# Three multiplications of the second attention on VectorE as two-tensor operations

## The reference

```python
def _L1_xattn_ref(latents, context, Wq, Wk, Wv, Wo, q_norm_w, k_norm_w):
    kv = jnp.concatenate([context, latents], axis=1)          # 64 + 256 keys
    q = (latents @ Wq).reshape(bsz, q_len, HEADS, HEAD_DIM).transpose(0, 2, 1, 3)
    k = (kv @ Wk).reshape(bsz, kv_len, KV_HEADS, HEAD_DIM).transpose(0, 2, 1, 3)
    v = (kv @ Wv).reshape(bsz, kv_len, KV_HEADS, HEAD_DIM).transpose(0, 2, 1, 3)
    q = rms_norm(q, q_norm_w)
    k = rms_norm(k, k_norm_w)
    qg = q.reshape(bsz, KV_HEADS, groups, q_len, HEAD_DIM)
    scores = jnp.einsum('bhgqd,bhkd->bhgqk', qg, k) * scale
    probs = jax.nn.softmax(scores.astype(jnp.float32), axis=-1).astype(q.dtype)
    out = jnp.einsum('bhgqk,bhkd->bhgqd', probs, v)
    ...
    return out @ Wo
```

## Time and profile before

| what | value |
|---|---|
| median of three runs | 1533.31 us (1529.5 to 1533.53) |
| profiled execution, first to last instruction | 1532.8 us |
| PE busy | 1433.3 us, 94% |
| DVE busy | 1135.0 us, 74% |
| ACT busy | 756.9 us, 49% |
| POOL busy | 517.1 us, 34% |
| mean granted TensorE clock | 0.990 |

### The profile page before, as it was taken

One profiled execution on the slowest core, in us unless ns is written; L12 is line 12 of the kernel. 1 busy time (PEld: TensorE's weight loads), 2 busy tenths in 40 slices (PEclk: granted clock), 3 DMA queues, 4 the chain that ended last, 5 costly groups with the idle time before them and its releaser, 6 DMA issues. The chain is left out here.

```text
span 1532.8 us, 24378 instructions
## 1 busy us (share of the span) xinstructions
PE 1433.3 (94%) x8064; PEld 1209.6 (79%) x8064; DVE 1135.0 (74%) x2870; ACT 756.9 (49%) x2127; POOL 517.1 (34%) x586
## 2 busy tenths in 40 slices
PE   5999999999999998999999999999999999999889
PEld 4888888887778887787888878878878887877767
DVE  7888888888641426778788788787787787786765
ACT  5666666667220314545545554554555555455521
POOL 4733333443691722232132132132132222322110
PEclk9999999999999999999999999999999999999979
DMA  4111111120230300100101001001001001010001
GB/s 186 70 66 45 68 55 68 68 68 1 83 112 28 131 18 1 69 1 15 56 1 68 0 0 68 0 0 68 0 0 68 0 0 68 19 35 1 1 1 55
DMA packets 14933, 63.75 MB, mean 42 GB/s; under 512 B 1760, under 2 KB 1760, under 8 KB 10656
## 3 DMA queue, kind: packets, MB, share of 16 engines
q1 hardware_dynamic: 14880, 63.07, 11.6%
HBM read 60.97 MB, written 2.10 MB: 41 GB/s over the span
## 5 line engine op out<-in xcount | busy, mean ns | idle before, releaser
L1183 ACT ACTIVATE p<-psum,nb,rq 128x320 f32<-128x320 f32 x256 | 155.5, 614 | 208.1 <-DVE nb L997 208.0
L55 PE MATMUL psum<-w1q_hi,xnT_lo 128*128 128x512 f32 x256 | 108.9, 425 | 7.7 <-DVE v_lo L1017 4.3
L993 DVE TENSOR_REDUCE mx<-psum 128x2 f32<-128x640 f32 x128 | 105.0, 820 | 9.4 <-PE psum L57 3.8
L962 DVE TENSOR_TENSOR pT_lo<-psum,pT_hi 128x512 fp32r<-128x512 f32 x128 | 88.0, 688 | 26.1 <-ACT pT_hi L1126 24.0
L923 POOL TENSOR_TENSOR rk<-ssk,rms_eps 128x3 f32<-128x3 f32 x32 | 6.2, 195 | 296.6 <-DVE ssk L1031 296.6
L243 POOL TENSOR_TENSOR p<-p,rinv 128x256 f32<-128x256 f32 x64 | 39.2, 613 | 193.0 <-DVE rinv L319 193.0
L434 ACT ACTIVATE p<-psum,nb 128x64 f32<-128x64 f32 x256 | 76.8, 313 | 50.7 <-DVE nb L344 50.6
L56 PE MATMUL psum<-w1q_lo,xnT_hi 128*128 128x512 f32 x256 | 101.4, 396 | 0.0
L57 PE MATMUL psum<-w1q_hi,xnT_hi 128*128 128x512 f32 x256 | 101.2, 395 | 0.0
L55 PE MATMUL psum<-w1o_hi,oT_lo 128*128 128x512 f32 x256 | 100.9, 394 | 0.0
L56 PE MATMUL psum<-w1o_lo,oT_hi 128*128 128x512 f32 x256 | 100.6, 393 | 0.0
(11 more groups left out here) (249 smaller groups left out, 4827.5 us busy)
## 6 DMA issues: line engine op xcount, KB each, us to landing
raw_q<-in_w0q SPq DMA_DIRECT2D x8, 1024.0 KB, 4.8
raw_o<-in_w0o SPq DMA_DIRECT2D x8, 1024.0 KB, 4.8
raw_q<-in_w1q SPq DMA_DIRECT2D x8, 1024.0 KB, 7.6
raw_o<-in_w1o SPq DMA_DIRECT2D x8, 1024.0 KB, 4.9
raw_kv<-in_w_gu SPq DMA_DIRECT2D x10, 512.0 KB, 3.6
raw_gu<-in_w_gu SPq DMA_DIRECT2D x10, 512.0 KB, 3.6
raw_kv<-in_w0kv SPq DMA_DIRECT2D x8, 515.0 KB, 3.3
raw_kv<-in_w1kv SPq DMA_DIRECT2D x8, 512.0 KB, 5.6
```

Source lines behind the costliest of these rows:

```text
L55: pe.matmul(out, w[1], m[0], start=start, stop=False)
L962: last = dve.tensor_tensor(k.pT[1][:, kt, 2 * hp:2 * hp + 2, :], bank.rearrange("p (h q) -> p h q", h=2), f(k.pT[0][:, kt, 2 * hp:2 * hp + ...
L993: dve.tensor_reduce(k.mx[:, stat(j)], s_pair(j), AX.X, ALU.max).then_inc(mx_ready, 1)
L1183: last = act.activation(k.p1[:, tile, h, :], s_pair(j)[:, h % 2, :], ACT.Exp, bias=k.nb[:, i:i + 1], scale=k.rq[:, i:i + 1], accum_out=k.r ...
```

## The change

Three things on DVE in attention 1. The maximum is reduced with its sign turned (`negate=True`, tile `neg_mx` in place of `mx`), and its product with `rq` is a tensor_tensor of two elements in place of a scalar_tensor_tensor. The two tensor_scalar operations of 320 elements that scale a pair of heads of p become one tensor_tensor of 640 elements with `rinv` repeated along the keys (`over_keys`). The two or three tensor_scalar operations of 128 elements on `k_raw` become one tensor_tensor of 256 or 384 elements with `rk` repeated. POOL's `p_scale` is written with the same helper and does what it did. Waits, semaphore counts and the order of the work stay.

```diff
--- before.py
+++ after.py
@@ -810,7 +810,7 @@
     k.p1 = sb(scope, "p1", [2, GH, SEQ + CTX])
     k.dump, k.rms_eps = sb(scope, "dump", [2 * GH + 3, HD]), sb(scope, "rms_eps", [2 * GH])
     k.ssk, k.rk = sb(scope, "ssk", [3]), sb(scope, "rk", [3])
-    k.ssq, k.rq, k.mx, k.nb, k.rs, k.rinv = (sb(scope, n, [2 * GH]) for n in ("ssq", "rq", "mx", "nb", "rs", "rinv"))
+    k.ssq, k.rq, k.neg_mx, k.nb, k.rs, k.rinv = (sb(scope, n, [2 * GH]) for n in ("ssq", "rq", "neg_mx", "nb", "rs", "rinv"))
 
 
 def attn1_phase(nc, k, sem, ln):
@@ -880,6 +880,9 @@
         tile, hp = PAIRS[j]
         return slice(tile * GH + 2 * hp, tile * GH + 2 * hp + 2)
 
+    def over_keys(ap):
+        return ap.unsqueeze(2).to_broadcast([PART, 2, KEYS])
+
     def loop(eng, body, tail):
 
         body(0, True, True)
@@ -913,8 +916,7 @@
                 tile, hp = PAIRS[j]
                 p = k.p1[:, tile, 2 * hp:2 * hp + 2, :]
                 pool.wait_ge(rinv_ready, 4 * n + j + 1)
-                pool.tensor_tensor(p, p, k.rinv[:, stat(j)].unsqueeze(2).to_broadcast([PART, 2, KEYS]),
-                                   ALU.mult).then_inc(p_scaled_pool, 1)
+                pool.tensor_tensor(p, p, over_keys(k.rinv[:, stat(j)]), ALU.mult).then_inc(p_scaled_pool, 1)
 
             def body(g, first, nxt):
                 for b in range(BATCH):
@@ -990,12 +992,11 @@
 
             def row_max(n, j):
                 dve.wait_ge(s_full, 4 * n + j + 1)
-                dve.tensor_reduce(k.mx[:, stat(j)], s_pair(j), AX.X, ALU.max).then_inc(mx_ready, 1)
+                dve.tensor_reduce(k.neg_mx[:, stat(j)], s_pair(j), AX.X, ALU.max, negate=True).then_inc(mx_ready, 1)
                 if j == 0:
                     dve.wait_ge(rq_ready, n + 1)
                 dve.wait_ge(mx_ready, 4 * n + j + 1)
-                dve.scalar_tensor_tensor(out=k.nb[:, stat(j)], in0=k.mx[:, stat(j)], scalar=-1.0, in1=k.rq[:, stat(j)],
-                                         op0=ALU.mult, op1=ALU.mult).then_inc(nb_ready, 1)
+                dve.tensor_tensor(k.nb[:, stat(j)], k.neg_mx[:, stat(j)], k.rq[:, stat(j)], ALU.mult).then_inc(nb_ready, 1)
 
             def scale_p(n, j):
                 tile, hp = PAIRS[j]
@@ -1004,10 +1005,8 @@
                 if j == 0:
                     return
                 dve.wait_ge(rinv_ready, 4 * n + j + 1)
-                for h in (2 * hp, 2 * hp + 1):
-                    last = dve.tensor_scalar(k.p1[:, tile, h, :], k.p1[:, tile, h, :],
-                                             k.rinv[:, tile * GH + h:tile * GH + h + 1], None, ALU.mult)
-                last.then_inc(p_scaled, 1)
+                p = k.p1[:, tile, 2 * hp:2 * hp + 2, :]
+                dve.tensor_tensor(p, p, over_keys(k.rinv[:, stat(j)]), ALU.mult).then_inc(p_scaled, 1)
 
             def body(g, first, nxt):
                 for b in range(BATCH):
@@ -1040,9 +1039,9 @@
                     if prev:
                         t_lo(n, b, 1)
                     dve.wait_ge(rk_ready, n + 1)
-                    for i in range(nk):
-                        last = dve.tensor_scalar(k.k_raw[:, i, :], k.k_raw[:, i, :], k.rk[:, i:i + 1], None, ALU.mult)
-                    last.then_inc(k_scaled, 1)
+                    k_raw = k.k_raw[:, 0:nk, :]
+                    dve.tensor_tensor(k_raw, k_raw, k.rk[:, 0:nk].unsqueeze(2).to_broadcast([PART, nk, HD]),
+                                      ALU.mult).then_inc(k_scaled, 1)
                     if prev:
                         t_lo(n, b, 2)
                         t_lo(n, b, 3)
```

## The result

| kernel | median, us | lowest to highest | ratio to before, 95% interval |
|---|---|---|---|
| before | 1533.22 | 1529.5 to 1533.53 | |
| after | 1559.53 | 1558.07 to 1560.92 | 1.0171 (1.0158 to 1.0183) |

The changed kernel is 26.3 us slower. The forecast was 1529.9 and the range ended at 1540, so it had both the sign and the size wrong. The profiled execution of the changed kernel has a span of 1559.1 us and a granted clock of 0.981.

A forecast was written before the change was run, and what follows sets the result against it. It took PE to set the pace, with DVE mattering only where PE waits for it. Span 1532.8 - 5.0 (b = 3 into b = 0) + 1.6 (b = 1) = 1529.4, median 1529.9 us; range 1519 to 1540.

The forecast's parts named there:

- Part 3: k scaling on DVE: single operations of 384 and 256 elements take 0.55 and 0.41 us quiet, gaining 3.2 us in all.
- the Sum: Profiled span 1532.8 - 5.0 + 1.6 = 1529.4 us, with the median 0.5 us above it: 1529.9.
- C: Rival: the 640-element p scaling takes 0.3 us above 0.82 and overruns DVE's slack, 1540.2 us; chance 0.15.
- rival A: The forecast itself: 1529.9 us, own range 1525 to 1534; chance 0.50.
- three signs that would have shown it wrong: Quiet 640-element scaling over 0.95 us, L986's stalls staying 8, or the b = 3 product falling behind POOL's last piece.
- Part 1: The two-element product as tensor_tensor on DVE, with the sign in the reduction: 0 us, bounds -0.01 and +0.12 each.
- Part 2: p scaling on DVE: one 640-element operation takes 0.82 us quiet against 0.68 for the pair, 13.4 us of DVE in all.
- Part 4, b = 3 into b = 0: Group's fourth unit into the next group's first: the one p scaling waits for one POOL piece; 7 x 0.72 = -5.0 us.
- rival E: The change moves only hidden work, nothing gained at b = 3: 1533 us; chance 0.12.
- Part 4, b = 1: Group's second unit: one k scaling wins 0.9 us, given back when q's squares meet POOL pieces, 0.2 more: +1.6 us.
- Rival B: No give-back at b = 1, as the second square does not meet POOL's fourth piece: 1522.3 us; chance 0.17.
- D: Rival: the new form of the scalings does not wait for POOL, 1515.8 us; chance 0.06.

The follow-up runs named there:

- after_pad24: The changed kernel with 24 one-column DVE memsets added in feed-forward 0, ahead of the loop; 1530.07 us, ratio 0.9975.
- after_pad1: The changed kernel with one one-column DVE memset added in feed-forward 0, ahead of the loop; 1528.3 us in one execution.
- product_only: The kernel before with only the negated maximum and the two-element tensor_tensor product of the change, both scalings as before; 1534.8 us, ratio 1.0007.
- p_only: The kernel before with only the change's p scaling and product, k scaled as before; 1527.18 us, ratio 0.9957.
- k_only: The kernel before with only the change's k scaling and product, p scaled as before; 1532.61 us, ratio 0.999.
- before_pad72: The kernel before with 72 one-column DVE memsets added in feed-forward 0, ahead of the loop; 1554.34 us, ratio 1.0132.
- split_o: The changed kernel with 8 memsets, and POOL's four w1o_lo pieces at b = 1 put two behind rk and two behind rq; 1524.98 us, ratio 0.9941.

## Why the prediction was wrong, step by step

**The step that failed.** Part 3 says "No DMA or queue order is touched, and no wait is added", and the Sum takes the spans of operations alone. The change touches one more stream: it takes 54 DVE instructions out of the list, 18 of them ahead of the loop, and this moves the loop's start from 17 behind a block's edge to one ahead of the next. The loop is shorter than before and yet reaches into a fourth block. The term that was missing is 867.8 - 836.1 = 31.7 us of attention time (after against after_pad24), 6.3 for each of the five branches back. The starts of v_lo in both traces split it. The five units that end with a stop are 23.7 us longer in sum, about PE's five waits for v_lo (23.9). The five units behind a stop are 9.4 longer, 1.3 to 2.7 each: the second runs from 915.82 to 945.40 in after and from 906.28 to 933.20 in after_pad24. There PE has its stretch of half clock, 21 matmuls in 7 us where 38 follow at full speed. And 1.7 comes back in the unit b = 2 of the last group, where after_pad24 has a stretch of half clock and after has none.

None of the rivals had this mechanism. C, the one on the slow side, decides from 0.95 us a scaling, and the quiet scaling is 0.825. The layout could have been priced: a loop of 291 instructions touches four blocks from 34 of the 128 possible offsets. But nothing in the profile of before shows a reload (its queue row has 23 packets), and the 58 in the offset came only from after and after_pad1.

**What held.** With the layout put right the forecast of the operations stands: after_pad24 takes 1530.07 us against the 1529.9 of rival A, span 1529.7 against 1529.4. An agreement to 0.2 us is luck in part: the +1.6 us of b = 1 was not there, two stretches of half clock that come and go between these layouts are worth 0.6 and 1.6 us, and after_pad1 with the same operations took 1528.3. None of the three signs that would have shown it wrong came up. Its steps:

- Part 1, the product at nothing: 0.160/0.161 us against 0.161 before, and product_only at 1.0007.
- Part 2, 0.82 us quiet: 0.825, so rival C is out. DVE's extra time did not reach PE: no unit of p_only is longer than the same unit of before by more than 0.05 us.
- Part 3, 0.55 and 0.41 us quiet: 0.558 and 0.417.
- Part 4, b = 3 into b = 0: the scaling at 1.945 us (1.95), the product in the third piece, not behind the last, and PE's transposes at b = 0 later by 0.2 to 0.3 us (0.81 us of wait in place of 0.62), while the waits for v_lo and then pT_lo go. DVE of after_pad24, then PE:

```profile
899.16 1.94 DVE L1012 TENSOR_TENSOR p<-p,rinv 128x640 f32<-128x640 f32 x1
902.53 0.98 DVE L1002 TENSOR_TENSOR nb<-neg_mx,rq 128x2 f32<-128x2 f32 x1
905.56 1.09 PE L1231 MATMUL psum<-ident,p 128*128 128x128 f32 x8 [0.81 <-DVE p L1012]
906.75 0.50 PE L55 MATMUL psum<-w1q_hi,xnT_lo 128*128 128x512 f32 x1
```

- Forecast -5.0 us for these; p_only's attention is 7.2 us shorter, after_pad24's 4.7. Both have some 0.6 of it from the clock in the first unit. In the unit b = 2 of the last group, from 1394.01 to 1426.28 in before, p_only is another 1.4 shorter and after_pad24 0.2 longer: this is the clock too. The chain that the forecast priced at 5.0 is what is left, 5.2 in p_only and 4.3 in after_pad24. With 0.9957 for p_only, rival E is out.
- Part 4, b = 1, the 0.9 us given back: it was. POOL, DVE and PE of after_pad24:

```profile
827.89 5.26 POOL L915 TENSOR_TENSOR w1o_lo<-raw_o,w1o_hi 128x512 fp32r<-128x512 f32 x4
827.95 1.51 DVE L1046 TENSOR_TENSOR k_raw<-k_raw,rk 128x256 f32<-128x256 f32 x1 [0.64 <-POOL rk L930]
830.99 1.01 DVE L991 CUSTOM_DVE_ANT_0 dump<-q_raw 128x128 f32<-128x128 f32 x1
831.93 1.37 DVE L991 CUSTOM_DVE_ANT_0 dump<-q_raw 128x128 f32<-128x128 f32 x1
831.12 0.66 PE L1231 MATMUL psum<-ident,p 128*128 128x128 f32 x4 [0.29 <-DVE pT_lo L967]
834.39 0.44 PE L1316 MATMUL psum<-ident,k_raw 128*128 128x128 f32 x2 [0.54 <-DVE pT_lo L967]
835.27 0.66 PE L1325 MATMUL psum<-ident,q_raw 128*128 128x128 f32 x4 [0.45 <-DVE pT_hi L971]
```

One scaling meets one piece and takes 1.51 us, so PE's transposes wait 0.29 where two scalings had them wait far longer. But two of the squares are held, 1.01 and 1.37 us, where before one was (16 in all, as forecast, where before has 8), and PE waits 0.54 and 0.45 us behind them. The forecast had 0.5 us at L1231 and 1.2 at L1325 (its L1229 and L1323); it came to 0.29 and 0.45, and the 0.54 at the transposes of k, L1316, it had not named. The net was put at +1.6 us for eight groups; k_only, with 0.0 of attention time, says that nothing is lost beyond the 0.9. So this term was too large by 1.6. Rival B is out, since both squares stall, and so is D, since the scalings wait.

## What to carry to other kernels

Count an edit's instructions, not only their time: inside or ahead of a loop they move its start against the blocks in which code is loaded, and a loop that reaches into a fourth block is loaded anew at each branch back, here (blocks of 128 instructions, six passes) for 30 us of 1530. So when a change comes out some per cent slower with its operations as fast as forecast, look at the row of the instruction queue and for "issue" idle time at the head of the loop, and shift the loop with a few idle instructions before the edit is judged. And where two engines take turns, moving one operation out of a turn pays only if what follows it doesn't walk into the next one: here the k scaling paid only once POOL's pieces were parted.

## What the runs showed of the hardware that I had not expected

- A single DVE instruction, a memset of one column over 100 us ahead of the loop, decides over 31 us (1559.53 against 1528.3). One load that is waited for takes 2.3 to 2.6 us of DVE, two take 4.4 to 5.0.
- A stop of PE can cost more than its length. Behind all five waits of 3.0 to 3.3 us in before_pad72 and all five of 4.6 to 4.9 in after PE got the level of 1.2 GHz for a good part of the next 7 us: the granted clock there is 0.63 to 0.65 in before_pad72, and 0.74, 0.59, 0.78, 0.63 and 0.80 in after. Behind a wait of 1.7 us, in the unit b = 2 of the last group, it goes either way: the same wait and the same four transposes (PE's timeline) in before, in after_pad24 and in after_pad1:

```profile
1400.92 1.09 PE L1229 MATMUL psum<-ident,p 128*128 128x128 f32 x4 [1.73 <-DVE pT_lo L962]
```

```profile
1397.31 1.09 PE L1231 MATMUL psum<-ident,p 128*128 128x128 f32 x4 [1.74 <-DVE pT_lo L967]
```

```profile
1396.78 0.63 PE L1231 MATMUL psum<-ident,p 128*128 128x128 f32 x4 [1.73 <-DVE pT_lo L967]
```

  1.09 us for four is the lower level, 0.63 the full clock (granted 0.76 and 1.00 from 1397 to 1404 us in after_pad24 and after_pad1). The profile shows nothing else that differs in the work around them, and why is open. It is worth 1.6 us: this unit lasts 32.5 us in after_pad24 and 30.9 in after_pad1. The other 0.9 of the 2.5 us of attention time between the two (836.1 and 833.6) gathers over the groups before, and no run shows why.
- An operation that waits for POOL's piece gets its turn between two pieces that stand directly behind each other, and not only when POOL's list runs dry; the piece that waits in turn ends later by less than the operation took: in split_o two pieces need 2.73 us beside the k scaling of 256 elements (0.417 us when quiet) and 2.53 without it. The 0.20 is what the forecast had for it.
